# Attention loops on one core: the value products of chunk n-2 are issued directly behind the scores by key of chunk n, ahead of the scores for the maxima

## The reference, cut to what matters

```python
# layer 1 and layer 5 (all keys are seen by all queries)
probs = softmax(q_h @ k_h.T * scale); out_h = probs @ v_h
# layer 7 (latent attention, causal; each head also has 64 rotary features)
scores = (q_h @ k_h.T + rope(qr_h) @ rope(kr).T) * scale
probs = softmax(where(causal, scores, -inf)); out_h = probs @ v_h
```

## Time and profile before

| | us |
|---|---|
| median of 3 runs (1413.32 to 1418.07) | 1414.84 |
| the profiled execution | 1413.13 |
| its span | 1411.1 |
| PE busy | 1325.0 (94%) |
| DVE busy | 893.1 (63%) |
| ACT busy | 689.3 (49%) |
| POOL busy | 278.5 (20%) |

### The profile page before, as it was taken

The page is one execution under the profiler, slowest core; times in us unless marked ns, Lnnn a source line. Parts: engine busy times, 40 slices in busy tenths (PEclk is TensorE's granted clock), DMA queues, the critical chain, the costliest instruction groups (busy, mean ns, idle before and its releaser), DMA issues. The chain is left out here.

```text
span 1411.1 us, 33212 instructions
## 1 busy us (share of the span) xinstructions
PE 1325.0 (94%) x13887; PEld 741.7 (53%) x13895; DVE 893.1 (63%) x2159; ACT 689.3 (49%) x1038; POOL 278.5 (20%) x343
## 2 busy tenths in 40 slices
PE   8999998999679988999999989999899999989999
PEld 4455554475346774644555554446355555654436
DVE  5999993757486456759999736433656556526431
ACT  5678786636483226546777842111444444442110
POOL 5340522001420000052000000111533434200110
PEclk9999999999889989999999999999999999999999
DMA  4323300000300000032222030001200000000000
GB/s 98 67 42 69 66 3 21 15 2 1 120 1 4 16 1 16 1 64 36 36 36 36 2 118 0 1 0 26 46 13 19 14 14 15 8 1 0 0 0 30
DMA packets 33526, 37.50 MB, mean 27 GB/s; under 512 B 8722, under 2 KB 24194, under 8 KB 33378
## 3 DMA queue, kind: packets, MB, share of 16 engines
q1 hardware_dynamic: 33376, 35.38, 12.2%
q10 hardware_dynamic: 2, 0.00, 0.0%
HBM read 18.43 MB, written 1.07 MB: 14 GB/s over the span
## 5 line engine op out<-in xcount | busy, mean ns | idle before, releaser
L677 DVE TENSOR_REDUCE row_max_pieces<-psum 128x1 f32<-128x512 f32 (+3 forms) x672 | 406.9, 646 | 103.2 <-PE psum L565 101.2
L778 ACT ACTIVATE probs<-psum 128x1024 f32<-128x1024 f32 (+7 forms) x384 | 343.4, 900 | 199.9 <-PE psum L565 199.4
L624 PE MATMUL psum<-probs,v_ones 128*32 128x256 f32 (+1 forms) x2880 | 236.4, 362 | 8.8 <-POOL probs L554 4.4
L565 PE MATMUL psum<-q_all,k_head 97*32 97x512 f32 (+3 forms) x1536 | 176.9, 487 | 0.0
L565 PE MATMUL psum<-k_stack,q_stack 96*32 96x512 bf16 x2048 | 159.8, 379 | 3.3 <-issue 3.2
L565 PE MATMUL psum<-q_stack,k_stack 97*32 97x512 bf16 x2048 | 158.0, 379 | 2.0 <-issue 1.8
L624 PEld LDWEIGHTS psum<-probs,v_ones 128*32 128x32 f32 x2880 | 95.5, 109 | 87.7 <-POOL probs L554 24.3
L565 PEld LDWEIGHTS psum<-k_stack,q_stack 96*32 96x32 bf16 x2048 | 57.7, 95 | 65.6 <-DVE row_max_pieces L677 12.2
L565 PE MATMUL psum<-k_head_bf,q_all_bf 80*32 80x512 bf16 (+3 forms) x768 | 84.0, 328 | 3.3 <-ACT k_head_bf L2625 1.0
L565 PEld LDWEIGHTS psum<-q_stack,k_stack 97*32 97x32 bf16 x2048 | 58.5, 96 | 51.7 <-ACT probs L778 4.3
L565 PEld LDWEIGHTS psum<-q_all,k_head 97*32 97x32 f32 x1536 | 75.8, 109 | 18.0 <-issue 2.6
(11 more groups left out here) (380 smaller groups left out, 2060.8 us busy)
## 6 DMA issues: line engine op xcount, KB each, us to landing
q_stack<-arena SPq DMA_DIRECT2D x32, 96.0 KB, 2.7
k_stack<-arena SPq DMA_DIRECT2D x32, 96.0 KB, 3.0
arena<-gd_g_sums SPq DMA_DIRECT2D x6, 512.0 KB, 6.0
k_stack<-arena SPq DMA_DIRECT2D x32, 64.0 KB, 2.6
q_stack<-arena SPq DMA_DIRECT2D x32, 64.0 KB, 2.7
x_tokens<-in_x SPq DMA_DIRECT2D x4, 256.0 KB, 3.8
k_stack<-arena SPq DMA_DIRECT2D x32, 32.0 KB, 2.2
q_stack<-arena SPq DMA_DIRECT2D x32, 32.0 KB, 2.7
```

The costliest lines, as they stand in the source:

```text
L565: last = pe.matmul(o[j:j + 32], by[:, j:j + 32], rows, **flags)
L624: last = pe.matmul(psum[32 * g:32 * g + VW, PVB, first * P:end * P].rearrange("p (b n) -> p b n", n=P), V[:, c, h, :], by_group(pr[:, n % ...
L677: last = dve.reduce_max(mx[:, h % 2, qt, i:i + 1], o[:, 0:plain], AX.X)
L778: act.activation(pr[:, n % PB, q_from(c):], psum[:, 2 * (n % 2):2 * (n % 2) + 2, :].rearrange("p a n -> p (a n)")[:, q_from(c):], ACT.Exp, ...
```

## The change

In the loop over chunks, `values(n - LAG)` moves from the end of the chunk to directly behind `key_scores(n)`. No instruction, wait or size is changed, and the streams of DVE, ACT, POOL and SP stay as they are.

```diff
                 for n in range(CHUNKS):
                     key_scores(n)
+                    if n >= LAG:
+                        values(n - LAG)
                     if n + LEAD < CHUNKS:
                         max_scores(n + LEAD)
                     if n % NT == 3:
                         turn(n // NT + 1)
                     if rope and n % NT == rope.AT and n // NT + rope.AHEAD < HEADS:
                         rope_in(n // NT + rope.AHEAD)
-                    if n >= LAG:
-                        values(n - LAG)
```

## The result

The changed kernel takes 1426.5 us (median of 4 runs, 1423.68 to 1432.12) against 1414.08 us for the one before (4 runs, 1410.27 to 1418.07): ratio 1.0094, 95% interval 1.0055 to 1.0132. The forecast was 1429.5 us and slower. The profiled execution has a span of 1422.1 us against 1411.1.

A forecast was written before the change was run, and what follows sets the result against it. PE was taken to bound the heads; 10.0 + 5.2 = 15.2 us on the profiled 1413.1 gave 1428.3, or 1430.0 with the median's 1.7 above it. The forecast was 1429.5 us, range 1421.5 to 1436.

The forecast's parts named there:

- What bounds the kernel: Loops over heads: PE full in non-causal layers, 10.4 us of blocks and 0.58 at the turn making 11.0 a head.
- The order of the other blocks is free: All three loops: moving values that need not wait for another engine costs nothing.
- Term 1: Non-causal layers: values of c = 0 wait for `keep_out`, 0.37 us an ordinary head, 0.43 with magnitudes; 10.0 us.
- Term 2: Causal layer, twelve changes of heads: one maxima block falls outside POOL's mask chain, 0.43 us each; 5.2 us.
- The sum: Whole kernel: 10.0 + 5.2 = 15.2 us slower, forecast as 1429.5 us.
- Only magnitudes and POOL: Rival: ordinary waits are swallowed, only heads with magnitudes and the POOL term count; 7.8 us, 1422.6; chance 0.08.
- Nothing: Rival: matmuls behind a waiting one overtake it, so the maxima block fills the wait; 1413 to 1417; chance 0.06.
- Faster: Rival: in the causal layer, values issued ahead fill maxima blocks' waits for the ring; 1408 to 1409; chance 0.05.
- The clock: Rival: PE's granted clock falls from 2.4 to 1.2 GHz in some heads; +10 for one head, 1440; chance 0.03.

The follow-up runs named there:

- run 3: Changed kernel, but non-causal values of c = 0 and causal values of c = 7 back behind the maxima block; ratio 1.0013 to the kernel before.
- run 5: Changed kernel, but non-causal values of c = 0 and causal values of c = 6 and c = 7 back behind their maxima blocks; 1413.62 us.
- run 8: Kernel of run 6, but causal values of c = 3 back behind the rotary products; 1409.96 us.
- run 6: Changed kernel, with POOL's rotary halves and ACT's magnitudes one chunk later; 1412.49 us.
- run 7: Kernel before the change, with POOL's rotary halves and ACT's magnitudes one chunk later; 1403.58 us, ratio 0.992.
- run 9: Changed kernel, with values three chunks back instead of two; 1407.7 us.
- run 4: Changed kernel, but non-causal values of c = 7 and causal values of c = 6 back behind the maxima block; 1439.3 us.

## Why the prediction was right

- **What bounds the kernel.** Right. PE is full in the non-causal heads from head 1 on, and each 0.36 us of wait lengthened the head by 0.34 us; the turn still stands 0.57 us behind the block ahead of it (720.74 to 721.31). The working of the 11.0 us comes out by luck. It counts the 0.43 us of the block ahead of the turn twice, once in the 24 blocks and once in the 0.58, and leaves out the 0.43 from the turn (726.07) to the next block:

```profile
726.50 0.64 PE L624 MATMUL psum<-probs,v_ones 128*32 128x256 f32 x8
```

- **The order of the other blocks is free.** Right to 0.05 us a head for the non-causal layers (run 3: 11.05 with seven of eight moved), and for the causal one but for the three values of c = 3, 6 and 7 (runs 5 and 8).
- **Term 1**, 10.0 us. The waits were as forecast: 0.37 for an ordinary head and 0.34 to 0.35 measured, 0.43 for a head with magnitudes and 0.41 to 0.43 measured, 9.3 us over the 26 heads. But the two loops grew by only 8.6 us (4.42 + 4.16). The prediction left out head 0. There PE is not full, but waits at the turn for DVE's maxima, and the block of values that now stands ahead of the turn fills this wait. The first turn of the loop in the first layer and then in the fifth, before:

```profile
53.96 0.27 PE L591 MATMUL psum<-identity,minus_max 128*8 128x128 f32 x1 [0.20 <-DVE row_max_pieces L677]
...
649.29 0.27 PE L591 MATMUL psum<-identity,minus_max 128*8 128x128 f32 x1 [0.18 <-DVE row_max_pieces L677]
```

  And after:

```profile
54.05 0.27 PE L591 MATMUL psum<-identity,minus_max 128*8 128x128 f32 x1 [0.19 <-DVE row_max_pieces L677]
...
653.48 0.27 PE L591 MATMUL psum<-identity,minus_max 128*8 128x128 f32 x1
```

  In the first layer this turn stands 11.51 us behind turn 0 in both kernels, although it now has a block more (0.43 us) ahead of it; in the fifth layer the distance grows by 0.19 us (11.32 to 11.51) instead of 0.43. That gives back some 0.7 us in all.

- **Term 2**, 5.2 us: 0.43 a head forecast, 0.42 to 0.46 measured at the twelve changes, and 5.4 us from first to closing turn. The steps held: the chain still ends 2.16 us behind the values of c = 6, and a maxima block stands outside it. What I had not seen is that there is a second loss of 0.2 us at the ring, hidden under POOL's chain (PE would wait there either way) and laid bare by runs 6 to 8. The changed kernel shows it too, at 1147.51 in the timeline above. And in the expectation of run 3 I took the block behind the values of c = 7 for the cause by itself, although the prediction's own 2.19 us say that only one of two blocks fits.
- **The sum.** 15.2 us forecast and 14.0 measured from first to closing turn: term 1 too large by 1.4 and term 2 too small by 0.2. That the turns give 15.4 is no better agreement, since 1.4 of it is the block that changed its side of the ruler. The difference of the medians is 12.4 us; 14.0 us would be a ratio of 1.0099, inside the interval. The rest is within what the stretches outside the loops do from run to run. Term 1's and term 2's causes are shown by the runs; that the median came out 3.0 us under the forecast is not evidence on them.
- **The rivals.** Only magnitudes and POOL: no, ordinary heads pay (11.35). Nothing: no matmul overtook the waiting values (719.00, then 719.43). Faster: not in the causal layer, where the waits of PE for the ring are not filled but grow (run 6); a small gain of this kind, 0.7 us in the two heads 0, is in the sum. The clock: 1.00 in these stretches in both profiles.

## What to carry to other kernels

Where one engine is full, permuting its blocks cost next to nothing here (0.05 us a head at most) except at the few that wait for another engine; so list those waits, find how much later the waited-for thing ends than the new place, and add that up. A block issued ahead of a waiting one is cover, and two waits on one chain must be moved together or the cover only changes ends. When consumers stand too close to their producers, more distance (here a third chunk back, run 9) or a producer that serves the urgent thing first (the mask before the rotary half, run 7) takes the wait away: each of the two runs is faster in its loops than the kernel before, run 9 in spite of the new order. And where a change moves blocks past the instruction that serves as ruler, measure the sum to one that has the same work ahead of it.

## What the runs showed of the hardware

What lies outside the turns took 858 to 879 us in the profiles of the different runs, of which at most 1.4 us is the block that stands on one side of the last turn or the other, while the mean distance of the turns inside the loops repeated to 0.02 us between kernels with the same order; 0.05 us a head could be told from a single profile, and 6 us could not be told from single times. From the end of ACT's copy to the start of the matmul that waited for it took 0.14 to 0.15 us in the three places read (119.74 to 119.89 before, 718.86 to 719.00 after, 723.71 to 723.85 in run 4).
